# Attention kernel on one core: projection blocks move to odd units, and a fixed set of units copies both halves on ScalarE

## The chip, the core and the metric

The kernel runs on one core of a Trainium2 chip. The time is the device time of one execution in microseconds (us). The five engines work through their own instruction lists in parallel and wait for each other by semaphores: TensorE (PE; its weight loads are listed apart as PEld), VectorE (DVE), ScalarE (ACT), GpSimd (POOL), and SyncE (SP), which issues nearly all DMAs.

## The reference

`x` is 8 × 1024 × 256, `adj` 1024 × 1024. Four residual layers follow one another, each on h = relu(layernorm(x)):

```
x = x + (adj @ h) @ W0 + b0                         # graph layer 0
x = x + norm_adj @ (h @ W1) + b1                    # graph layer 1
x = x + o + layernorm(o),  o = attention_2(h) @ w_proj + b_proj
                                                    # 8 heads of 32, scores masked where adj == 0
x = x + attention_3(h) @ Wo + bo                    # 8 heads of 32, scores + (1 - adj) * -1e9
```

Everything is fp32. Products that need its precision are split into a high and a low part.

## The kernel before, in words

`graph_phase` computes the first two layers and takes the first 480 us; the change does not touch it. `attention_phase` computes the two attention layers in 16 **jobs** (8 batches for each layer). A job has 8 heads of 8 query tiles, so 64 **units** `u`; a unit is one tile of 128 queries against all 1024 keys of one head.

In unit `u` the engines do this, each in the order of its own loop:

- TensorE: `scores` of unit u+2 (two matmuls of 128x512, L720); the unit's **block** if it has one; in even units the `values` of two steps (L751, 16 matmuls that multiply the probabilities of the head before with V); then `transposes` of unit u (L732, eight of 128x128, in two halves of four; each half has its own bank of `pt_ps`).
- VectorE: `masked` for unit u+2 (L939: scores plus mask, and the row's smallest value); the second part of the block (`finish_block`); `copy_pt` of the second half of the transposes (L1014), if ScalarE doesn't do it.
- ScalarE: `exp` for unit u+1 (L870); every 16 units, from u = 7 on, `copy_ot` (L881); `copy_pt` of the first half (L875), and of the second where it is ScalarE's; the first part of the block (`hi_part`).

So each half of `pt_ps` must be copied before the next unit's transposes write it again, and `values` at every eighth unit also needs the first half of the unit before.

A **block** is one piece of projection work that is spread over the units of the attention: `h` and `turn` and `norm` are four transposes; `qk`, `v` and `out` are six matmuls of 512 columns or twelve of 256. All blocks go through one bank, `g_ps`: a block may start when VectorE has finished the one before (`g_free`). For `h`, `turn` and `qk` ScalarE writes the high part first (L852, L864, L860) and VectorE then the low part (L950, L988, L957); `norm`, `v` and `out` have no part on ScalarE. Which unit holds which block is written out by hand in three tables: `EARLY` (the rest of the job before), `MID` (this job), `NEXT` (the job after). The first job has no `EARLY`, the last no `NEXT`. SyncE waits for some blocks as well: the loads of head 4 wait for the fourth `qk` of `MID`, those of the next job's head 0 for the last of `NEXT`.

Before the change ScalarE copies both halves in 19 of the 64 units: those with a `v`, `norm` or `out` block, and of the units without a block those with u % 4 == 3 except u % 16 == 7. In a unit with an `h` or `turn` block the copies stand ahead of the block's own work on ScalarE and VectorE, with any other block behind it.

Of the kernel before, what the change touches and what calls it, by code (L numbers as in the profile page):

```python
# [37 lines left out]
def graph_phase(nc, a, x_mid, mask, shared):  # L38
# [14 lines left out]
    with ExitStack() as ctx:  # L53
# [235 lines left out]
        def _(dve):  # L289
# [124 lines left out]
UNITS = 64  # L414
GROUP = 2
EARLY = [(9, ("norm", 3)), (11, ("turn", 0)), (13, ("out", 0)), (15, ("turn", 1)), (17, ("out", 1)),
         (26, ("turn", 2)), (28, ("out", 2)), (30, ("turn", 3)), (32, ("out", 3))]
MID = [(18, ("qk", 1, 0, 0)), (20, ("qk", 1, 1, 0)), (22, ("qk", 1, 0, 1)), (24, ("qk", 1, 1, 1)),
       (33, ("norm", 0)), (49, ("norm", 1)), (60, ("norm", 2))]
NEXT = [(35, ("h", 0, 0)), (37, ("h", 0, 1)), (40, ("h", 1, 0)), (42, ("h", 1, 1)),  # L420
        (44, ("v", 0)), (45, ("v", 1)), (47, ("v", 2)), (48, ("v", 3)),
        (51, ("qk", 0, 0, 0)), (53, ("qk", 0, 1, 0)), (54, ("qk", 0, 0, 1)), (56, ("qk", 0, 1, 1))]

FIRST = [("h", 0, 0), ("h", 0, 1), ("h", 1, 0), ("h", 1, 1),
         ("qk", 0, 0, 0), ("qk", 0, 1, 0), ("qk", 0, 0, 1), ("qk", 0, 1, 1), ("v", 0), ("v", 1), ("v", 2), ("v", 3)]
# [2 lines left out]
SHORT = ("h", "turn")  # L428
LN_STEP = 16
PER_JOB = len(EARLY) + len(MID) + len(NEXT)  # L430


def blocks_of(first, more):

    table = sorted((EARLY if not first else []) + MID + (NEXT if more else []))
    skip = len(EARLY) if first else 0
    return {step: (skip + i, what) for i, (step, what) in enumerate(table)}


def scalar_halves(table):  # L440


    return {u for u in range(UNITS)
            if (table[u][1][0] in ("v", "norm", "out") if u in table else u % 4 == 3 and u % 16 != 7)}


def attention_phase(nc, a, x_mid, x_mid2, out, mask, shared):
# [11 lines left out]
    with ExitStack() as ctx:  # L459
# [102 lines left out]
        def block_at(job, k):  # L562

            return PER_JOB * job + FIRST_BLOCKS - len(EARLY) + k
# [13 lines left out]
        def tail_block(k):  # L578
            return block_at(JOBS, k) - len(NEXT)

        banks = [g_ps, pt_ps[0], pt_ps[1], ot_ps]

        def bank(k):

            return banks[0 if k is None else k % 4]
# [113 lines left out]
        def _(pe):  # L699
# [108 lines left out]
            def body(job, layer, before, after):  # L808
                table = blocks_of(before is None, after is not None)
                for u in range(UNITS):  # L810
                    if u + 2 < UNITS or after is not None:
                        scores(job, u + 2, UNITS * job + u + 1)
                    if u in table:
                        k, what = table[u]
                        lay = before if (u, what) in EARLY else after if (u, what) in NEXT else layer
                        if what[0] == "norm":
# [25 lines left out]
        @block.scalar  # L842
        def _(act):
            copy = nc.scalar.activation

            def hi_part(n, what, layer, job, k=None, last=False):

                kind, ps = what[0], bank(k)
                if kind == "h":
                    c, nh = what[1:]  # L850
                    act.wait_ge(g_mm, n + 1)
                    copy(hT_hi[:, c, nh * HALF:(nh + 1) * HALF], ps[:], ACT.Relu).then_inc(h_hi_done, 1)  # L852
                elif kind == "qk":
                    g, w, nh = what[1:]
                    if not (g == 0 and job == 0):

                        for s in range(2):
                            act.wait_ge(head_in[s], 128 * (4 * job + 2 * g))
                    act.wait_ge(g_mm, n + 1)
                    copy(st_hi[w][:, nh * HALF:(nh + 1) * HALF], ps[:], ACT.Identity,  # L860
                         bias=b_qk[:, layer, w, g:g + 1]).then_inc(qk_hi_done, 1)
                elif kind == "turn":
                    act.wait_ge(g_mm, n + 1)
                    copy(oT(what[1], last)[0], ps[:], ACT.Copy).then_inc(oT_hi_done, 1)  # L864

            def exp(job, u):
                job, u = (job + 1, u - UNITS) if u >= UNITS else (job, u)

                act.wait_ge(t_done, UNITS * job + u + 1)
                nc.scalar.activation(T[u % RING][:], T[u % RING][:], ACT.Exp, bias=low[:, u % RING:u % RING + 1],  # L870
                                     scale=-1.0, accum_out=rsum[:, u:u + 1]).then_inc(p_done, 1)

            def copy_pt(job, u, half):
                act.wait_ge(tr_done[half], UNITS * job + u + 1)
                copy(pt_of(u, half),  # L875
                     pt_ps[half][:].rearrange("p (k q) -> p k q", k=HT), ACT.Copy).then_inc(pt_done[half], 1)

            def copy_ot(after):

                act.wait_ge(av_done, after)  # L880
                copy(ot_sb[:], ot_ps[:], ACT.Copy).then_inc(ot_done, 1)  # L881

            def weights_hi(layer):
                if layer:
                    act.wait_ge(raw_in, 64)
                raw = raw_weights(layer)

                copy(w_hi[layer][:, :, 0:D], raw[:, :, 0:D], ACT.Copy, scale=-SCALE).then_inc(w_hi_done, 1)
                copy(w_hi[layer][:, :, D:], raw[:, :, D:], ACT.Copy).then_inc(w_hi_done, 1)

            weights_hi(0)
            act.wait_ge(bias_zero, 1)
            for n, what in enumerate(FIRST):
                hi_part(n, what, 0, 0, n)
            weights_hi(1)
            act.wait_ge(bias_done, 1)
            exp(0, 0)

            def body(job, layer, before, after):
                table = blocks_of(before is None, after is not None)  # L900
                for u in range(UNITS):
                    if u + 1 < UNITS or after is not None:
                        exp(job, u + 1)
                    if u % (2 * NT) == NT - GROUP + 1 and (u >= NT or before is not None):
                        copy_ot(UNITS * job + u + GROUP - 1 - NT)
                    halves = (0, 1) if u in scalar_halves(table) else (0,)
                    copy_first = u in table and table[u][1][0] in SHORT
                    if copy_first:
                        for half in halves:
                            copy_pt(job, u, half)  # L910
                    if u in table:
                        k, what = table[u]
                        in_next = (u, what) in NEXT
                        hi_part(block_at(job, k), what, after if in_next else layer, job + 1 if in_next else job)
                    if not copy_first:
                        for half in halves:
                            copy_pt(job, u, half)

            jobs(body)
            copy_ot(UNITS * JOBS)  # L920

            for i in range(2):
                act.wait_ge(head_in[i], 128 * 4 * JOBS)
            for k, what in enumerate(LAST):
                hi_part(tail_block(k), what, 1, None, k, True)
# [3 lines left out]
        def _(dve):  # L929
# [82 lines left out]
            def copy_pt(job, u):  # L1012
                dve.wait_ge(tr_done[1], UNITS * job + u + 1)
                nc.vector.tensor_copy(pt_of(u, 1),  # L1014
                                      pt_ps[1][:].rearrange("p (k q) -> p k q", k=HT)).then_inc(pt_done[1], 1)
# [38 lines left out]
            def body(job, layer, before, after):  # L1054
                table = blocks_of(before is None, after is not None)
                for u in range(UNITS):
                    if u + 2 < UNITS or after is not None:
                        masked(job, u + 2, layer if u + 2 < UNITS else after)
                    copy_first = u in table and table[u][1][0] in SHORT
                    if copy_first and u not in scalar_halves(table):  # L1060
                        copy_pt(job, u)
                    if u in table:
                        k, what = table[u]
                        early, in_next = (u, what) in EARLY, (u, what) in NEXT
                        finish_block(block_at(job, k), what, before if early else after if in_next else layer,
                                     job - 1 if early else job + 1 if in_next else job)
                    if not copy_first and u not in scalar_halves(table):
                        copy_pt(job, u)
                    if after is not None:
                        if LN_STEP <= u < LN_STEP + NT:  # L1070
                            ln_stats(job + 1, u - LN_STEP)
                        if u == LN_STEP + NT:
                            ln_mean(job + 1)
                    if layer != after and after is not None and u >= UNITS - NT + 1:
                        mask3(u - (UNITS - NT + 1))
                        if u == UNITS - 1:
                            mask3(NT - 1)
# [139 lines left out]
```

## Time and profile before

| | us |
|---|---|
| median of 3 runs | 2976.08 (2975.07 to 2977.13) |
| the profiled execution | 2974.42, its span 2972.6 |
| TensorE busy | 2906.1 (98%) |
| VectorE busy | 2401.1 (81%) |
| ScalarE busy | 2126.1 (72%) |
| GpSimd busy | 591.3 (20%) |

The granted TensorE clock has a mean of 0.994 of full speed. The line numbers L... are those of the kernel before. Matmuls are pipelined, so their durations overlap: how long a piece of TensorE's work takes is read from the start of one row to the start of the next. A unit is measured here from the start of its scores (L720) to the start of the next unit's scores. Job 3 runs from 960.53 to 1113.70 us.

### The profile page before, as it was taken

To read this page: it belongs to the slowest core of one execution; us is meant where nothing else is said; L and a number is where in the kernel's file an instruction comes from. 1 tells how busy PE (TensorE), PEld (TensorE's weight loads), DVE (VectorE), ACT (ScalarE), POOL (GpSimd) and SP (SyncE) were. 2 spreads that over 40 slices of the span, in tenths; PEclk is the share of its full clock that TensorE was granted. 3 is DMA by queue.
4 is the path that set the end of the run, shared out by engine and by line. 5 is a ranking of instruction groups with operands and counts; after the bars stand their busy time and mean duration, and the time that the engine had idled before them with its cause. 6 is when DMAs were issued, how large, how long until landed. Compare 5 with 4: busy or idle time off the path is not lost.

```text
span 2972.6 us, 59755 instructions
## 1 busy us (share of the span) xinstructions
PE 2906.1 (98%) x23872; PEld 2199.0 (74%) x23872; DVE 2401.1 (81%) x4427; ACT 2126.1 (72%) x3794; POOL 591.3 (20%) x538
## 2 busy tenths in 40 slices
PE   7999997999999999999999989999999999999998
PEld 6888886777777777777777767777777777777776
DVE  6776775879888888888888878888888787878786
ACT  3000002888888888888888878888888888888887
POOL 2222220105050504131322323010101010101000
PEclk9999998999999999999999999999999999999999
DMA  3001003323233233232323252323233332323232
GB/s 124 29 29 58 29 29 94 70 56 90 69 83 75 71 74 83 65 93 61 96 51 97 67 140 68 90 66 85 65 81 74 82 76 72 87 55 93 65 75 58
DMA packets 123588, 217.19 MB, mean 73 GB/s; under 512 B 20016, under 2 KB 88240, under 8 KB 123312
## 3 DMA queue, kind: packets, MB, share of 16 engines
q1 hardware_dynamic: 122160, 209.14, 28.4%
q0 software_dynamic: 1152, 4.19, 0.6%
q8 instruction: 195, 3.19, 0.4%
q14 instruction: 81, 0.66, 0.1%
HBM read 53.87 MB, written 25.17 MB: 27 GB/s over the span
## 4 chain that ended last, share of the span: by engine, by line
PE 79%; ACT 2%; DVE 1%; DMA 1%; issue 0%; ACTq 0%; DVEq 0%
PE t_pt_ps L732 32%; PE t_ot_ps L751 17%; PE t_s_ps L720 15%; PE t_g_ps L705 4%; PE t_g_ps L706 4%; PE t_g_ps L707 4%; PE t_g_ps L772 1%; PE t_g_ps L776 1%; PE t_g_ps L791 1%; ACT t_T L870 1%; ACT t_PT L875 1%; DMA mask<-in_adj 1%; DVE t_st_lo L957 0%; ACT t_st_hi L860 0%; ACT t_ot L881 0%
## 5 line engine op out<-in xcount | busy, mean ns | idle before, releaser
L939 DVE CUSTOM_DVE_ANT_0 t_T<-t_s_ps,mask 128x1024 f32<-128x1024 f32 x1024 | 1240.6, 1215 | 117.3 <-PE t_s_ps L720 112.5
L870 ACT ACTIVATE t_T<-t_T,t_low 128x1024 f32<-128x1024 f32 x1024 | 1178.8, 1151 | 43.1 <-DVE t_low L939 37.9
L732 PEld LDWEIGHTS t_pt_ps<-t_ident,t_T 128*128 128x128 f32 x8192 | 885.2, 141 | 325.7 <-issue 279.5
L732 PE MATMUL t_pt_ps<-t_ident,t_T 128*128 128x128 f32 x8192 | 1112.6, 279 | 6.3 <-DVE t_PT L1014 4.5
L875 ACT ACTIVATE t_PT<-t_pt_ps 128x512 f32<-128x512 f32 x1324 | 755.9, 596 | 317.9 <-PE t_pt_ps L732 306.7
L720 PE MATMUL t_s_ps<-t_k,t_q 128*128 128x512 f32 x2048 | 729.7, 437 | 8.3 <-DMA t_k<-t_st_lo 7.1
L1014 DVE COPY t_PT<-t_pt_ps 128x512 f32<-128x512 f32 x724 | 499.1, 689 | 196.6 <-PE t_pt_ps L732 194.0
L751 PE MATMUL t_ot_ps<-t_PT,shared 128*32 128x256 f32 x8192 | 549.4, 386 | 8.1 <-ACT t_PT L875 7.9
L751 PEld LDWEIGHTS t_ot_ps<-t_PT,shared 128*32 128x32 f32 x8192 | 215.1, 109 | 255.4 <-issue 128.0
L247 ACT ACTIVATE g_yT_hi<-g_ps 128x512 fp32r<-128x512 f32 x64 | 38.3, 598 | 400.5 <-PE g_ps L187 400.5
L720 PEld LDWEIGHTS t_s_ps<-t_k,t_q 128*128 128x128 f32 x2048 | 310.6, 192 | 9.3 <-DMA t_k<-t_st_lo 7.6
L1108 POOL COPY shared<-shared 128x1024 f32<-128x1024 f32 x16 | 17.0, 1062 | 1263.8 <-PE t_ot_ps L751 1254.0
L185 PE MATMUL g_ps<-g_adjT_hi,g_h_hi 128*128 128x512 f32 x512 | 200.8, 392 | 7.2 <-DVE g_spare L362 5.6
L870 ACT ACTIVATION_READ_ACCUMULATOR t_T<-t_T,t_low 128x1 f32 x1024 | 200.6, 196 | 0.0
L186 PE MATMUL g_ps<-g_adjT_lo,g_h_hi 128*128 128x512 f32 x512 | 200.3, 391 | 0.0
L187 PE MATMUL g_ps<-g_adjT_hi,g_h_lo 128*128 128x512 f32 x512 | 199.9, 390 | 0.0
L957 DVE SCALAR_TENSOR_TENSOR t_st_lo<-t_g_ps,t_b_qk,t_st_hi 128x512 fp32r<-128x512 f32 x125 | 93.8, 750 | 66.1 <-ACT t_st_hi L860 65.1
L860 ACT ACTIVATE t_st_hi<-t_g_ps,t_b_qk 128x512 fp32r<-128x512 f32 x125 | 85.9, 687 | 42.9 <-PE t_g_ps L707 42.9
L185 PEld LDWEIGHTS g_ps<-g_adjT_hi,g_h_hi 128*128 128x128 f32 x512 | 96.7, 189 | 26.8 <-DVE g_spare L362 5.8
L187 PEld LDWEIGHTS g_ps<-g_adjT_hi,g_h_lo 128*128 128x128 f32 x512 | 96.6, 189 | 20.1
L186 PEld LDWEIGHTS g_ps<-g_adjT_lo,g_h_hi 128*128 128x128 f32 x512 | 96.7, 189 | 19.0
L705 PE MATMUL t_g_ps<-t_hT_hi,t_w_hi 128*128 128x512 f32 x250 | 100.7, 403 | 7.6 <-DVE t_st_lo L957 4.8
(185 smaller groups left out, 3158.1 us busy)
## 6 DMA issues: line engine op xcount, KB each, us to landing
t_q<-t_st_hi SPq DMA_DIRECT2D x256, 128.0 KB, 2.3
t_k<-t_st_hi SPq DMA_DIRECT2D x256, 128.0 KB, 2.4
t_k<-t_st_lo SPq DMA_DIRECT2D x256, 128.0 KB, 2.4
t_q<-t_st_lo SPq DMA_DIRECT2D x256, 128.0 KB, 2.4
shared<-x_after_graph_layers SPq DMA_DIRECT2D x8, 1024.0 KB, 6.5
t_xe<-x_after_graph_layers SPq DMA_DIRECT2D x32, 256.0 KB, 3.1
x_after_layer<-t_xe SPq DMA_DIRECT2D x32, 256.0 KB, 2.1
shared<-x_after_layer SPq DMA_DIRECT2D x8, 1024.0 KB, 6.8
```

The costliest lines, as they stand in the source:

```text
L185: mm(out, s_hi, m_hi, start=first, stop=False)
L186: mm(out, s_hi, m_lo, start=False, stop=False)
L187: return mm(out, s_lo, m_hi, start=False, stop=final)
L705: mm(dst, s_hi, m_hi, start=first, stop=False)
L706: mm(dst, s_hi, m_lo, start=False, stop=False)
L720: last = mm(s_ps[u % 2][:, cols], q4[h % 2][:, qt * P:(qt + 1) * P], k4[h % 2][:, cols], start=True, stop=True)
L732: last = nc.tensor.transpose(pt_ps[half][:, i * P:(i + 1) * P], T[u % RING][:, kt * P:(kt + 1) * P], ident[:])
L751: last = mm(ot_ps[j * HD:(j + 1) * HD, h % 2 * 2 * P:(h % 2 + 1) * 2 * P], v_sb[:, kt, h * HD:(h + 1) * HD], probs, start=kt == 0, stop=kt ...
L870: nc.scalar.activation(T[u % RING][:], T[u % RING][:], ACT.Exp, bias=low[:, u % RING:u % RING + 1], scale=-1.0, accum_out=rsum[:, u:u + 1] ...
L875: copy(pt_of(u, half), pt_ps[half][:].rearrange("p (k q) -> p k q", k=HT), ACT.Copy).then_inc(pt_done[half], 1)
L939: nc.vector.tensor_tensor_reduce(out=T[u % RING][:], in0=s_ps[u % 2][:], in1=mask[:, qt, :], scale=1.0, scalar=3.4e38, op0=ALU.add, op1=AL ...
L1014: nc.vector.tensor_copy(pt_of(u, 1), pt_ps[1][:].rearrange("p (k q) -> p k q", k=HT)).then_inc(pt_done[1], 1)
```

## The change

The tables get new unit numbers. Before, 15 of the 28 blocks of a full job stand in even units: 18, 20, 22, 24, 26, 28, 30, 32, 40, 42, 44, 48, 54, 56 and 60. After it three do: 18 (`qk`), 48 (`norm`) and 54 (`qk`). The rule for ScalarE's second halves is replaced by a written set of 32 units. The order within a unit changes too: in even units a block's work stands ahead of the copies on ScalarE and VectorE, whatever its kind; in odd units it stands behind the copies on VectorE, and on ScalarE behind the first copy (`h`, `turn`) or behind all (`qk`).

```diff
-         (26, ("turn", 2)), (28, ("out", 2)), (30, ("turn", 3)), (32, ("out", 3))]
-MID = [(18, ("qk", 1, 0, 0)), (20, ("qk", 1, 1, 0)), (22, ("qk", 1, 0, 1)), (24, ("qk", 1, 1, 1)),
-       (33, ("norm", 0)), (49, ("norm", 1)), (60, ("norm", 2))]
-NEXT = [(35, ("h", 0, 0)), (37, ("h", 0, 1)), (40, ("h", 1, 0)), (42, ("h", 1, 1)),
-        (44, ("v", 0)), (45, ("v", 1)), (47, ("v", 2)), (48, ("v", 3)),
-        (51, ("qk", 0, 0, 0)), (53, ("qk", 0, 1, 0)), (54, ("qk", 0, 0, 1)), (56, ("qk", 0, 1, 1))]
+         (25, ("turn", 2)), (27, ("out", 2)), (29, ("turn", 3)), (31, ("out", 3))]
+MID = [(18, ("qk", 1, 0, 0)), (19, ("qk", 1, 1, 0)), (21, ("qk", 1, 0, 1)), (23, ("qk", 1, 1, 1)),
+       (33, ("norm", 0)), (48, ("norm", 1)), (61, ("norm", 2))]
+NEXT = [(35, ("h", 0, 0)), (37, ("h", 0, 1)), (39, ("h", 1, 0)), (41, ("h", 1, 1)),
+        (43, ("v", 0)), (45, ("v", 1)), (47, ("v", 2)), (49, ("v", 3)),
+        (51, ("qk", 0, 0, 0)), (53, ("qk", 0, 1, 0)), (54, ("qk", 0, 0, 1)), (55, ("qk", 0, 1, 1))]
+BOTH_ON_ACT = {0, 2, 7, 8, 9, 12, 13, 15, 16, 17, 20, 22, 24, 26, 27, 29, 30, 31, 33, 39, 41, 42, 43, 46, 47, 48,
+               50, 54, 56, 58, 61, 63}
...
-def scalar_halves(table):
-    return {u for u in range(UNITS)
-            if (table[u][1][0] in ("v", "norm", "out") if u in table else u % 4 == 3 and u % 16 != 7)}
...
@@ ScalarE, inside the loop over the units
-                    halves = (0, 1) if u in scalar_halves(table) else (0,)
-                    copy_first = u in table and table[u][1][0] in SHORT
...
+                    def hi_of(kinds):
+                        if u in table and table[u][1][0] in kinds:
+                            k, what = table[u]
+                            in_next = (u, what) in NEXT
+                            hi_part(block_at(job, k), what, after if in_next else layer, job + 1 if in_next else job)
+
+                    if u % 2 == 0:
+                        hi_of(SHORT + ("qk",))
+                    copy_pt(job, u, 0)
+                    if u % 2:
+                        hi_of(SHORT)
+                    if u in BOTH_ON_ACT:
+                        copy_pt(job, u, 1)
+                    if u % 2:
+                        hi_of(("qk",))
@@ VectorE, inside the loop over the units
-                    copy_first = u in table and table[u][1][0] in SHORT
-                    if copy_first and u not in scalar_halves(table):
+                    if u % 2 and u not in BOTH_ON_ACT:
                         copy_pt(job, u)
                     if u in table:
                         ...
-                    if not copy_first and u not in scalar_halves(table):
+                    if u % 2 == 0 and u not in BOTH_ON_ACT:
                         copy_pt(job, u)
```

The first place is TensorE from unit 25 of a full job on, where the third `turn` block (four transposes of `t_o`) stands. Before:

```order
L720 MATMUL t_s_ps<-t_k_1,t_q_1 128x512 x2
L732 MATMUL t_pt_ps<-t_ident,t_T 128x128 x8
L720 MATMUL t_s_ps<-t_k_1,t_q_1 128x512 x2
L776 MATMUL t_g_ps<-t_ident,t_o 128x128 x4
L751 MATMUL t_ot_ps<-t_PT,shared 32x256 x8
L732 MATMUL t_pt_ps<-t_ident,t_T 128x128 x8
```

After, from the scores of unit 25 on (the lines of the changed kernel are five lower here):

```order
L715 MATMUL t_s_ps<-t_k_1,t_q_1 128x512 x2
L771 MATMUL t_g_ps<-t_ident,t_o 128x128 x4
L727 MATMUL t_pt_ps<-t_ident,t_T 128x128 x8
L715 MATMUL t_s_ps<-t_k_1,t_q_1 128x512 x2
L746 MATMUL t_ot_ps<-t_PT,shared 32x256 x8
L727 MATMUL t_pt_ps<-t_ident,t_T 128x128 x8
```

The block now stands between scores and transposes of unit 25 and no longer between scores and `values` of unit 26.

The second place is ScalarE in the units 53 and 54, which both hold a `qk` block (`t_st_hi` is its high part, `t_T` the exponential, `t_PT` the copies, `t_ot` the copy of `ot`). Before:

```order
L870 ACTIVATE t_T,t_rsum<-t_T,t_low 128x1024
L860 ACTIVATE t_st_hi<-t_g_ps,t_b_qk 128x512
L875 ACTIVATE t_PT<-t_pt_ps 128x512
L870 ACTIVATE t_T,t_rsum<-t_T,t_low 128x1024
L860 ACTIVATE t_st_hi<-t_g_ps,t_b_qk 128x512
L875 ACTIVATE t_PT<-t_pt_ps 128x512
L870 ACTIVATE t_T,t_rsum<-t_T,t_low 128x1024
L881 ACTIVATE t_ot<-t_ot_ps 128x512
```

After:

```order
L865 ACTIVATE t_T,t_rsum<-t_T,t_low 128x1024
L870 ACTIVATE t_PT<-t_pt_ps 128x512
L855 ACTIVATE t_st_hi<-t_g_ps,t_b_qk 128x512
L865 ACTIVATE t_T,t_rsum<-t_T,t_low 128x1024
L855 ACTIVATE t_st_hi<-t_g_ps,t_b_qk 128x512
L870 ACTIVATE t_PT<-t_pt_ps 128x512 x2
L865 ACTIVATE t_T,t_rsum<-t_T,t_low 128x1024
L876 ACTIVATE t_ot<-t_ot_ps 128x512
```

In unit 53 the copy now stands ahead of the block's high part; in unit 54 the high part stays ahead and two copies follow instead of one.

The third place is VectorE in unit 53 and at the start of unit 54 (`t_st_lo` is the low part of a `qk` block, `ISA` the mask operation). Before:

```order
L957 SCALAR_TENSOR_TENSOR t_st_lo<-t_g_ps,t_b_qk,t_st_hi 128x512
L1014 COPY t_PT<-t_pt_ps 128x512
L939 ISA t_T,t_low<-t_s_ps,mask 128x1024
L939 ISA t_low 128x1
L957 SCALAR_TENSOR_TENSOR t_st_lo<-t_g_ps,t_b_qk,t_st_hi 128x512
L1014 COPY t_PT<-t_pt_ps 128x512
```

After:

```order
L1014 COPY t_PT<-t_pt_ps 128x512
L957 SCALAR_TENSOR_TENSOR t_st_lo<-t_g_ps,t_b_qk,t_st_hi 128x512
L939 ISA t_T,t_low<-t_s_ps,mask 128x1024
L939 ISA t_low 128x1
L957 SCALAR_TENSOR_TENSOR t_st_lo<-t_g_ps,t_b_qk,t_st_hi 128x512
```

The copy of unit 53 has moved ahead of the block's low part, and unit 54 has no copy on VectorE.

## Rows read from the trace of the kernel before

**Rows 1.** Busy times of the engines in job 3 (us, instructions, then clock and DMA)
```profile
960.53:1113.73 153.20, 152.43 (x1348) 112.68 (x1346) 130.69 (x242) 129.02 (x233) 43.20 (x43) 1.00 0.32 77
```
**Rows 2.** Timeline, TensorE's scores of units 2, 3, 4 (start, us, engine, instruction)
```profile
964.49 0.71 PE L720 MATMUL t_s_ps<-t_k,t_q 128*128 128x512 f32 x2
...
966.98 0.71 PE L720 MATMUL t_s_ps<-t_k,t_q 128*128 128x512 f32 x2
...
968.42 0.71 PE L720 MATMUL t_s_ps<-t_k,t_q 128*128 128x512 f32 x2
```
**Rows 3.** Timeline, TensorE's scores of units 10 and 12 (`turn` in 11)
```profile
981.07 0.71 PE L720 MATMUL t_s_ps<-t_k,t_q 128*128 128x512 f32 x2
...
985.33 0.71 PE L720 MATMUL t_s_ps<-t_k,t_q 128*128 128x512 f32 x2
```
**Rows 4.** Timeline, scores of units 24 (`qk`), 26 (`turn`) and 28
```profile
1016.00 0.70 PE L720 MATMUL t_s_ps<-t_k,t_q 128*128 128x512 f32 x2
...
1021.31 0.70 PE L720 MATMUL t_s_ps<-t_k,t_q 128*128 128x512 f32 x2
...
1025.67 0.71 PE L720 MATMUL t_s_ps<-t_k,t_q 128*128 128x512 f32 x2
```
**Rows 5.** Timeline, scores of units 44, 45 (`v`), 46, and 51 (`qk`), 52
```profile
1062.25 0.71 PE L720 MATMUL t_s_ps<-t_k,t_q 128*128 128x512 f32 x2
...
1066.16 0.71 PE L720 MATMUL t_s_ps<-t_k,t_q 128*128 128x512 f32 x2
...
1068.92 0.71 PE L720 MATMUL t_s_ps<-t_k,t_q 128*128 128x512 f32 x2
...
1082.34 0.72 PE L720 MATMUL t_s_ps<-t_k,t_q 128*128 128x512 f32 x2
...
1085.08 0.70 PE L720 MATMUL t_s_ps<-t_k,t_q 128*128 128x512 f32 x2
```
**Rows 6.** Timeline, all engines in units 53 and 54 (brackets: idle before, releaser)
```profile
1089.51 1.04 PE L732 MATMUL t_pt_ps<-t_ident,t_T 128*128 128x128 f32 x8
...
1089.79 0.69 ACT L860 ACTIVATE t_st_hi<-t_g_ps,t_b_qk 128x512 fp32r<-128x512 f32 x1 [0.66 <-PE t_g_ps L707]
...
1090.30 0.70 PE L720 MATMUL t_s_ps<-t_k,t_q 128*128 128x512 f32 x2
1090.37 0.59 ACT L875 ACTIVATE t_PT<-t_pt_ps 128x512 f32<-128x512 f32 x1
1090.51 0.75 DVE L957 SCALAR_TENSOR_TENSOR t_st_lo<-t_g_ps,t_b_qk,t_st_hi 128x512 fp32r<-128x512 f32 x1 [0.84 <-ACT t_st_hi L860]
...
1091.32 0.50 PE L705 MATMUL t_g_ps<-t_hT_hi,t_w_hi 128*128 128x512 f32 x1 [0.32 <-DVE t_st_lo L957]
...
1094.60 0.60 ACT L875 ACTIVATE t_PT<-t_pt_ps 128x512 f32<-128x512 f32 x1 [0.82 <-PE t_pt_ps L732]
...
1094.75 0.71 PE L720 MATMUL t_s_ps<-t_k,t_q 128*128 128x512 f32 x2
...
1095.09 1.14 ACT L870 ACTIVATE t_T<-t_T,t_low 128x1024 f32<-128x1024 f32 x1
```
**Rows 7.** Timeline, ScalarE's first copy of unit 7 and `values` of unit 8
```profile
976.80 0.59 ACT L875 ACTIVATE t_PT<-t_pt_ps 128x512 f32<-128x512 f32 x1
...
977.44 1.07 PE L751 MATMUL t_ot_ps<-t_PT,shared 128*32 128x256 f32 x16 [0.44 <-ACT t_PT L875]
```
**Rows 8.** Timeline, both halves copied by ScalarE in unit 9 (behind a block) and 28
```profile
980.28 1.04 PE L732 MATMUL t_pt_ps<-t_ident,t_T 128*128 128x128 f32 x8
...
980.91 1.09 ACT L875 ACTIVATE t_PT<-t_pt_ps 128x512 f32<-128x512 f32 x2
...
1029.39 1.09 ACT L875 ACTIVATE t_PT<-t_pt_ps 128x512 f32<-128x512 f32 x2 [1.00 <-PE t_pt_ps L732]
...
1030.13 1.06 PE L732 MATMUL t_pt_ps<-t_ident,t_T 128*128 128x128 f32 x8
```
**Rows 9.** DMA issues of the mask's reload between jobs 7 and 8
```profile
mask<-in_adj POOLq DMA_DIRECT2D x8, 512.0 KB, 10.5
```

More of the change, by code:

```diff
@@ L905, in body @@
                         copy_ot(UNITS * job + u + GROUP - 1 - NT)
-                    halves = (0, 1) if u in scalar_halves(table) else (0,)
-                    copy_first = u in table and table[u][1][0] in SHORT
[L908 to L917, printed above, removed]
+                    def hi_of(kinds):
[12 more added lines that the diff above has]
+                        hi_of(("qk",))
             jobs(body)
```

## The prediction

> **What bounds the kernel now.** I read the busy times of one whole job first, then TensorE's rows unit by unit, then the rows of all engines at the places where TensorE waits. In [rows 1] TensorE is busy for 152.43 of the 153.20 us of job 3, VectorE for 130.69 and ScalarE for 129.02. The jobs 1 to 14 are alike, but for 7 and 8 in which the mask is reloaded; so all of them are paced by TensorE, and the others have 22 and 24 us to spare. A job is 64 units: an even unit holds scores, two `values` and transposes, an odd one scores and transposes. A plain even unit takes 2.49 us from its scores to the next, a plain odd one 1.44, a plain pair 3.93 [rows 2].
>
> **Part 1: blocks move from even to odd units.** What a block costs depends on where it stands. A `turn` in an odd unit makes its pair 4.26 us [rows 3], so it costs 0.33; in an even unit the pair is 4.36 [rows 4], so 0.43. A `qk` in an even unit makes the pair 5.31 [rows 4], or +1.38; an odd unit with one takes 2.74 against 1.44 [rows 5], or +1.30. A `v` costs 3.91 − 2.49 = 1.42 in an even unit and 2.76 − 1.44 = 1.32 in an odd one [rows 2, 5]. So a move saves 0.10 for the short ones and `v`, 0.08 for `qk`, and for `out` I take the same. To odd units go four `qk`, two `out`, two `turn`, two `h`, one `norm` and two `v`; one `norm` goes to an even one (49 to 48): 6 × 0.08 + 5 × 0.10 + 2 × 0.10 − 0.10 = 1.08 us per full job. No row shows a longer row of odd blocks than two units, so a move might save nothing or twice as much; the rows at hand give the middle.
>
> **Part 2: what TensorE waits for.** Three waits are left in a full job.
> - Unit 8. `values` waits for ScalarE's copy of unit 7 [rows 7], which stands behind the copy of `ot`: the copy starts at 976.80, the matmul at 977.44 with 0.44 of wait shown, and the unit is about 0.5 longer than a plain one. Units 7 and 8 hold no block before or after, and the first half is copied at the same place. Unchanged.
> - Unit 40. The same geometry, but today the 0.43 of the `h` block lies between scores and `values` and hides all but some 0.08 of the wait. Moved to unit 39 it delays that unit's transposes by only 0.33, so 0.18 is left: +0.10. At 24 and 56 the block in front is a `qk` of 1.3, and nothing is left, as now.
> - Unit 54. Two `qk` blocks follow each other here (53, 54) in one bank, so the second waits until VectorE is through with the first. Today [rows 6]: the transposes of unit 53 start at 1089.51, ScalarE takes the block's high part at 1089.79, ahead of its copy (1090.37), VectorE takes the low part 0.72 later (1090.51), and the next block starts 0.81 after that (1091.32). Without the wait it would stand 0.55 behind the scores of 1090.30, so 0.47 is waited. In the changed kernel an odd unit's `qk` part comes behind its copy on ScalarE, and the copy needs four transposes that stand behind the block on TensorE. Behind a block the copy starts 0.63 after the transposes (980.28 to 980.91 [rows 8]), here at 1090.14; the high part follows 0.49 later (the distance from 1094.60 to 1095.09 [rows 6]) at 1090.63, the low part at 1091.35, the block at 1092.16. That is 0.84 us later than now, and unit 54 goes from 4.45 (1090.30 to 1094.75) to 5.29.
>
> Behind that block stand `values` and transposes of unit 54, the scores of 57 and the `qk` of 55, and all come 0.84 later. The block of 55 needs no more: from the block of 54 its bank is free after some 1.6 for the block, 0.28, 0.72 and 0.81, or 3.4 us, and TensorE comes to it after 3.43 + 0.55 = 3.98 (1091.32 to 1094.75, and its scores). The other odd `qk` (19, 21, 23, 51) get their high part late too, but the next block is two units off, 3.8 us for a chain of 2.65 (0.63 + 0.49 + 0.72 + 0.81). The DMA queue waits for the blocks of units 23 and 55 before it loads heads 4 and 0; these were 24 and 56, so it is earlier. The step at 54 costs 0 only if the high part passed a waiting copy, which the rows deny: the exponential of 1095.09 stood behind a copy that waited 0.82 (1094.60). VectorE's own copy of unit 53 now stands ahead of the low part; were it not over by then, another 0.6 would come on top, 1.5 in all. I take 0.84. A full job changes by -1.08 + 0.84 + 0.10 = -0.14 us, fourteen of them by -2.0.
>
> **Part 3: thirteen more second halves on ScalarE.** It copies both halves in 32 units instead of 19. At 0.49 each this is 6.4 us per job, of 24 it has to spare; where, matters. A pair holds two exponentials of 1.14 (1095.09) and two copies of 0.49, 3.26 us, with two more copies 4.24. A plain pair is 3.93. In the new table a pair with two extra copies holds a block in every full job (8/9, 12/13, 16/17, 26/27, 30/31, 42/43, 46/47), so it lasts 4.26 or more: it just fits. Tightest is an even unit with no block behind it. [rows 8] show one of today: two copies from 1029.39, the next unit's transposes at 1030.13 with no wait; its second copy starts at 1029.88, must be 0.64 ahead of the second half (976.80 to 977.44 [rows 7]), at 1030.52, and that half starts about 0.43 behind 1030.13, at 1030.56. So 0.04 is left, and I cost part 3 at nothing in full jobs. If the cover is gone, it is up to 0.1 in each of 17 even units, 1.7 us per job.
>
> The Trainium skill (Advanced Engine Details and Errata, "The Read-Write Bubble") says that instructions of ScalarE and VectorE do not overlap at their ends, which leaves a bubble between them. By it a copy would take its whole 0.60, a pair with two extra ones 2 × 1.14 + 4 × 0.60 = 4.68, and seven pairs per job would be 0.42 late: 47 us in sixteen jobs, near 3021. The rows speak against it: 0.49 from one to the next, for a copy of 0.60, and two copies in 1.09 (1029.39).
>
> **The first and the last job.** The set is fixed now, while these have fewer blocks. Job 0 lacks the early ones, and `values` up to unit 7, so ScalarE is its bound there: two more copies are 1.0 us, and its five double pairs without a block up to 0.2 each, another 1.0. With 0.7 saved and 0.94 lost as above, +2.2. Job 15 lacks the last ones: 0.6 saved, two pairs 0.2 late each: -0.2. Where the mask is reloaded (jobs 7, 8) TensorE stands still until DMAs land that took 10.5 us [rows 9], set off by work whose order stays: 0, within 1 us.
>
> **Sum.** -2.0 + 2.2 − 0.2 = 0.0 us. The profiled execution's own time is 2974.42 (its span 2972.6), 1.66 below the median of the runs, 2976.08. So 2974.4 on its scale and 2976 as a median.
>
> **Rivals.**
> 1. The wait at 54 does not grow, or the moves save 0.15 and not 0.10. For it: ScalarE is idle around 54, and the odd units' blocks stand between like rows. Against it: the order in which ScalarE takes them. The first form gives 15 × 0.84 = 12.6 us less, 2963.5; the second 15 × 0.5 = 8 less, 2968; both 2956.
> 2. Slower: ScalarE is late with the second half in even units where it copies both. It decides from 0.04 us on where no block follows (units 0, 2, 56, 58), from 0.4 to 1.4 where one does. If all 17 lost 0.05, 16 × 17 × 0.05 = 13.6 more: 2989.5; 0.1 each makes 3003. For it: the pairs that just fit. Against it: [rows 8].
> 3. The change does not do what it says: the blocks stand in odd units, but unit 54 takes the gain back. That is the forecast itself, with part 3 as work moved beside TensorE's.
>
> **How the numbers follow.** About 0.2% (6 us) is what a measurement of this kernel can tell from no change. A full job must be off by 0.4 us to get there, and my terms for one are good to some 0.2 to 0.3. The forecast gets 0.51. Rival 1 gets 0.27, all of it faster; rival 2 gets 0.22, with 0.02 of it for the rule on the bubble. The likeliest case alone lies between 2971 and 2981. To hold eight in ten the range takes in the first form of rival 1 and the milder one of rival 2: 2962 to 2990.
>
> **What would show it.** Full jobs of 152.8 to 153.3 us; pairs with an odd `turn` or `h` of 4.26; unit 54 at 5.3 with its block waiting for VectorE's low part; no wait of TensorE for second copies in full jobs; job 0 some 2 us longer. Wrong would be a unit 54 below 4.7, or plain pairs above 3.95.

## The result, and the profile after

| | us | runs |
|---|---|---|
| before | 2975.05 (2973.66 to 2978.96) | 12 |
| changed | 2967.97 (2966.1 to 2972.39) | 12 |

The ratio is 0.9975, with a 95% interval of 0.9967 to 0.9982: faster by 0.25%. That is inside the range, but the likeliest case was "no change" (2971 to 2981), and the changed kernel lies just below it. The profiled execution of the changed kernel has a span of 2965.0 us, 7.6 below the one before.

Where these 7.6 are is read job by job, each from the scores of its unit 1 to those of the next job's unit 1 (job 15 to its last scores), and then unit by unit:

| part | before | changed | difference |
|---|---|---|---|
| 12 full jobs (1 to 6, 9 to 14), each | 153.19 | 152.90 | -0.29, together -3.4 |
| jobs 7 and 8 (reload of the mask) | 160.32 + 159.82 | 155.36 + 159.11 | -5.7 |
| job 0 | 145.11 | 146.25 | +1.1 |
| job 15 | 133.33 | 132.99 | -0.3 |
| unit 1 of job 0 starts at | 511.5 | 512.1 | +0.6 |

The last line can't be put down to the change: a second profile of each kernel (e7, e4) has 512.8 and 511.5.

The busy times of job 3 answer to [rows 1]:

```profile
961.62:1114.52 152.90, 151.19 (x1347) 113.15 (x1346) 123.38 (x229) 135.18 (x246) 43.19 (x43) 1.00 0.32 75
```

VectorE lost 7.3 us per job and ScalarE took on 6.2 (129.02 to 135.18), but TensorE still sets the pace. The scores of units 1, 2, 24, 25 and 26 answer to [rows 4] and [rows 2]:

```profile
964.14 0.71 PE L715 MATMUL t_s_ps<-t_k,t_q 128*128 128x512 f32 x2
...
965.55 0.71 PE L715 MATMUL t_s_ps<-t_k,t_q 128*128 128x512 f32 x2
...
1018.15 0.70 PE L715 MATMUL t_s_ps<-t_k,t_q 128*128 128x512 f32 x2
...
1020.63 0.71 PE L715 MATMUL t_s_ps<-t_k,t_q 128*128 128x512 f32 x2
...
1022.40 0.71 PE L715 MATMUL t_s_ps<-t_k,t_q 128*128 128x512 f32 x2
```

The pair 24/25 now holds a `turn` in its odd unit and takes 4.25 us; a `turn` in an even unit made 4.36. But unit 1 takes 1.41, and a plain odd unit took 1.44 [rows 2]: that was not foreseen. Unit 54 answers to [rows 6], in all engines:

```profile
1089.71 1.04 PE L727 MATMUL t_pt_ps<-t_ident,t_T 128*128 128x128 f32 x8
...
1090.34 0.60 ACT L870 ACTIVATE t_PT<-t_pt_ps 128x512 f32<-128x512 f32 x1 [0.84 <-PE t_pt_ps L727]
1090.50 0.70 PE L715 MATMUL t_s_ps<-t_k,t_q 128*128 128x512 f32 x2
...
1090.84 0.68 ACT L855 ACTIVATE t_st_hi<-t_g_ps,t_b_qk 128x512 fp32r<-128x512 f32 x1
...
1091.55 0.75 DVE L957 SCALAR_TENSOR_TENSOR t_st_lo<-t_g_ps,t_b_qk,t_st_hi 128x512 fp32r<-128x512 f32 x1
...
1092.36 0.50 PE L700 MATMUL t_g_ps<-t_hT_hi,t_w_hi 128*128 128x512 f32 x1 [1.16 <-DVE t_st_lo L957]
...
1095.80 0.71 PE L715 MATMUL t_s_ps<-t_k,t_q 128*128 128x512 f32 x2
```

From the transposes 0.63 to the copy, 0.50 to the high part, 0.71 to the low part, 0.81 to the block. The wait shown grew from 0.32 to 1.16, the unit from 4.45 to 5.30. The list of waits of the whole execution has it 15 times (its total in us, how often, the longest), once in each job but the last:

```profile
PE t_g_ps L700 <- DVE t_st_lo L957: 17.4, 15, 1.2
```

The reload of the mask is where most of the gain is. GpSimd issues its eight DMAs behind `masked` of the units 56 to 63 of job 7, and `masked` of the next job waits for them. Windows of ten us from the first issue on, of before and then of the changed kernel (the last three columns are the granted clock, the share of the DMA engines and GB/s):

```profile
1706.08:1716.08 10.00, 10.00 (x94) 6.73 (x85) 8.05 (x14) 8.28 (x15) 2.74 (x4) 1.00 0.59 163
1716.08:1726.08 10.00, 6.85 (x58) 4.96 (x57) 6.15 (x12) 6.89 (x14) 2.28 (x4) 0.98 1.03 204
1726.08:1736.08 10.00, 8.79 (x63) 5.74 (x63) 7.23 (x12) 5.35 (x10) 1.03 (x1) 0.68 1.05 244
```
```profile
1705.35:1715.35 10.00, 10.00 (x95) 6.95 (x94) 6.55 (x11) 8.58 (x16) 2.35 (x4) 1.00 0.55 141
1715.35:1725.35 10.00, 8.74 (x84) 5.88 (x76) 8.62 (x16) 8.07 (x15) 2.92 (x5) 1.00 1.00 287
1725.35:1735.35 10.00, 6.71 (x58) 4.63 (x54) 5.13 (x9) 5.73 (x11) 0.29 (x1) 1.00 1.05 259
```

In both the DMA engines are full from the second window on, but in the second window of the changed kernel they move 287 GB/s and not 204; over the thirty us it is 229 and 204 in the mean. The fourth tile's issue on GpSimd and the mask operation that waits for it on VectorE, before:

```profile
1715.23 1.03 POOL L1155 DMA_DIRECT2D mask<-in_adj  x1 [3.03 <-DVE t_low L939]
...
1726.10 0.69 DVE L1020 TENSOR_SCALAR mask<-mask 128x1024 f32<-128x1024 f32 x1 [3.84 <-DMA mask<-in_adj]
```

and in the changed kernel:

```profile
1714.89 1.03 POOL L1154 DMA_DIRECT2D mask<-in_adj  x1 [0.98 <-DVE t_low L939]
...
1722.98 0.69 DVE L1020 TENSOR_SCALAR mask<-mask 128x1024 f32<-128x1024 f32 x1 [1.34 <-DMA mask<-in_adj]
```

10.9 us from issue to use became 8.1. The eighth tile is issued only when the fourth has let VectorE go on (2.13 us behind its use in both), so it comes sooner as well. It is what VectorE waits for last, before and then in the changed kernel:

```profile
1739.12 0.69 DVE L1020 TENSOR_SCALAR mask<-mask 128x1024 f32<-128x1024 f32 x1 [2.96 <-DMA mask<-in_adj]
```
```profile
1735.38 0.69 DVE L1020 TENSOR_SCALAR mask<-mask 128x1024 f32<-128x1024 f32 x1 [3.53 <-DMA mask<-in_adj]
```

Both kernels started unit 1 of job 7 at 1575.74, so 3.7 of the 5.7 us are won by then. Most of the rest is TensorE's clock. It fell from 2.4 to 1.2 GHz while TensorE stood idle behind this wait, and in the kernel before it stayed there twice as long as in the changed one (the third number from the end is the granted clock):

```profile
1739.39:1746.22 6.83, 4.60 (x26) 2.69 (x27) 5.23 (x9) 2.97 (x5) 0.00 (x0) 0.50 0.03 11
```
```profile
1737.08:1740.49 3.41, 3.22 (x19) 1.30 (x20) 3.02 (x7) 2.85 (x5) 0.00 (x0) 0.50 0.00 0
```

Before, the clock was at 1.2 GHz once more, from 1725.74 to 1732.57, but that stretch ended while the eighth tile was still on its way. So did TensorE's own longest waits for a DMA, which the profile puts down to the last load of `t_k` for the next job's head 0 (4.36 us up to 1727.29, and 1.26 up to 1723.70 in the changed kernel). The median time of the eight from issue to landing, in answer to [rows 9]:

```profile
mask<-in_adj POOLq DMA_DIRECT2D x8, 512.0 KB, 7.5
```

### The profile page after: what moved, and what is told of

It is laid out like the page before. It is cut to its first block, busy times and chain, and to the rows that moved or that the text cites. A ratio compares the mean times of both kernels' runs of the same rounds, so it can differ in the third digit from the quotient of the medians.

```text
span 2965.0 us, 59755 instructions
## 1 busy us (share of the span) xinstructions
PE 2886.2 (97%) x23872; PEld 2205.8 (74%) x23872; DVE 2283.8 (77%) x4215; ACT 2225.7 (75%) x4006; POOL 590.6 (20%) x538
## 4 chain that ended last, share of the span: by engine, by line
PE 77%; ACT 5%; DVE 1%; DMA 1%; issue 0%; ACTq 0%; DVEq 0%
PE t_pt_ps L727 31%; PE t_ot_ps L746 17%; PE t_s_ps L715 14%; PE t_g_ps L700 4%; PE t_g_ps L701 4%; PE t_g_ps L702 4%; ACT t_PT L870 2%; ACT t_T L865 2%; PE t_g_ps L767 1%; PE t_g_ps L771 1%; PE t_g_ps L786 1%; DMA mask<-in_adj 1%; ACT t_ot L876 1%; DVE t_st_lo L957 0%; ACT t_st_hi L855 0%
## 5 line engine op out<-in xcount | busy, mean ns | idle before, releaser
L727 PE MATMUL t_pt_ps<-t_ident,t_T 128*128 128x128 f32 x8192 | 1097.1, 277 | 3.0 <-ACT t_PT L870 1.7
L727 PEld LDWEIGHTS t_pt_ps<-t_ident,t_T 128*128 128x128 f32 x8192 | 897.8, 141 | 268.2 <-issue 226.2
L870 ACT ACTIVATE t_PT<-t_pt_ps 128x512 f32<-128x512 f32 x1536 | 870.0, 599 | 247.4 <-PE t_pt_ps L727 231.6
L1014 DVE COPY t_PT<-t_pt_ps 128x512 f32<-128x512 f32 x512 | 353.1, 690 | 200.8 <-PE t_pt_ps L727 200.6
L715 PEld LDWEIGHTS t_s_ps<-t_k,t_q 128*128 128x128 f32 x2048 | 310.2, 192 | 10.9 <-DVE t_low L939 4.8
```

Source lines behind the costliest of these rows:

```text
L715: last = mm(s_ps[u % 2][:, cols], q4[h % 2][:, qt * P:(qt + 1) * P], k4[h % 2][:, cols], start=True, stop=True)
L727: last = nc.tensor.transpose(pt_ps[half][:, i * P:(i + 1) * P], T[u % RING][:, kt * P:(kt + 1) * P], ident[:])
L870: copy(pt_of(u, half), pt_ps[half][:].rearrange("p (k q) -> p k q", k=HT), ACT.Copy).then_inc(pt_done[half], 1)
L1014: nc.vector.tensor_copy(pt_of(u, 1), pt_ps[1][:].rearrange("p (k q) -> p k q", k=HT)).then_inc(pt_done[1], 1)
```

## The experiments

All were timed beside the kernel before on the same chip, except e7. "Stall of the reload" is the length of jobs 7 and 8 together less two full jobs of the same profile; it was 13.8 before and 8.7 in the changed kernel.

**e1: only the tables.** The tables of the changed kernel stand in the kernel before; its rule for second halves and its order stay.

```diff
-         (26, ("turn", 2)), (28, ("out", 2)), (30, ("turn", 3)), (32, ("out", 3))]
+         (25, ("turn", 2)), (27, ("out", 2)), (29, ("turn", 3)), (31, ("out", 3))]
```

> Only the three tables are those of the changed kernel; the rule for second halves and the order within a unit stay as before. Theory (each move saves 0.08 to 0.10 us, and the order within odd units is what costs 0.84 in unit 54): full jobs of 152.2 us (153.2 before, 152.9 changed), unit 54 at 4.45 as before and unit 40 at 2.67; the time some 15 us below the kernel before, 2960, and 7 below the changed kernel. Rival (the wait in unit 54 comes from the neighbourhood 53, 54, 55 in the new table, not from the order): unit 54 at 5.3, full jobs of 153.0, 2972.

2960.68 us, ratio 0.9949 (0.9936 to 0.9963). Full jobs of 152.33 (two of the twelve 152.63), unit 54 at 4.46, unit 40 at 2.68, stall of the reload 10.1. The theory holds: the moves alone are worth 0.85 us per job, and the other two parts of the change give 0.57 of it back. One thing was not in it: units 24 and 56 take 2.57 and not 2.49.

**e2: only the set.**

```diff
 def scalar_halves(table):
-    return {u for u in range(UNITS)
-            if (table[u][1][0] in ("v", "norm", "out") if u in table else u % 4 == 3 and u % 16 != 7)}
+    return BOTH_ON_ACT
```

> Only the set of units in which ScalarE copies both halves is the changed kernel's; tables and order are those of before. Theory (a blockless odd unit behind an even unit whose two halves ScalarE copies takes 1.41 instead of 1.44, as units 29 and 61 do before and 1, 3, 57 and 59 in the changed kernel): nine or ten more such units, full jobs of 152.9, and with 1.1 us more in job 0 a time of 2972. Rival (the set only moves idle time): full jobs of 153.2, time 2975 or up to 1 more. Rival (ScalarE comes late): waits of TensorE for L875, full jobs above 153.5.

2986.55 us, ratio 1.0036 (1.0024 to 1.0048): slower. The third theory has the length of the full jobs right, but not the wait. Units 21, 23, 25, 27, 31, 43 and 55 do fall to 1.41, so the 0.03 are real. But units 28, 32 and 44 take 4.23 to 4.25 and not 3.86 to 3.90, and full jobs 154.0 to 154.1. The rows of units 26 to 28:

```profile
1026.93 1.09 ACT L877 ACTIVATE t_PT<-t_pt_ps 128x512 f32<-128x512 f32 x2 [0.51 <-PE t_pt_ps L734]
...
1027.90 0.60 ACT L866 ACTIVATE t_oT_hi<-t_g_ps 128x512 fp32r<-128x512 f32 x1
1028.38 1.16 ACT L872 ACTIVATE t_T<-t_T,t_low 128x1024 f32<-128x1024 f32 x1
1028.49 0.72 PE L722 MATMUL t_s_ps<-t_k,t_q 128*128 128x512 f32 x2
1028.54 0.69 DVE L990 TENSOR_TENSOR t_oT_lo<-t_g_ps,t_oT_hi 128x512 fp32r<-128x512 f32 x1 [2.07 <-ACT t_oT_hi L866]
...
1029.29 0.39 PE L707 MATMUL t_g_ps<-t_w_hi,t_oT_hi 128*128 128x256 f32 x1
```

In unit 26 (a `turn`) both copies now stand ahead of the high part on ScalarE, which comes at 1027.90; VectorE's low part comes at 1028.54, and TensorE, which reaches the next block 0.55 behind the scores of 1028.49, can start it only at 1029.29. The late releaser is once more ScalarE's order ahead of a block, as in unit 54, and no wait for copies. The set was only fit for its own tables. The stall of the reload fell all the same, to 8.1, and the fourth tile needs 8.3 us.

**e3: tables and set, but the old order within a unit.**

> Tables and set of the changed kernel, but the order within a unit of the kernel before: a qk block's high part ahead of the copies on ScalarE, its low part ahead of the copy on VectorE. Theory: unit 54 falls from 5.30 to about 4.46, full jobs from 152.9 to 152.1, 15 x 0.84 = 12.6 us less than the changed kernel, 2955. Rival (copies that come later in odd units cost TensorE elsewhere what 54 gains): full jobs stay at 152.8 to 153.0 and the time at 2968.

2967.98 us, ratio 0.9973 (0.9963 to 0.9983); full jobs of 152.87, stall of the reload 7.1. The theory falls, although its own part is there: unit 54 is back at 4.45. But units 24 and 56 take 2.77 (2.48 in the changed kernel), and unit 41 takes 2.00 (1.77): +0.81 together. The rows of units 23 and 24:

```profile
1017.10 0.59 ACT L883 ACTIVATE t_ot<-t_ot_ps 128x512 f32<-128x512 f32 x1
1017.10 1.03 PE L734 MATMUL t_pt_ps<-t_ident,t_T 128*128 128x128 f32 x8
1017.58 0.70 ACT L862 ACTIVATE t_st_hi<-t_g_ps,t_b_qk 128x512 fp32r<-128x512 f32 x1
...
1018.15 0.61 ACT L877 ACTIVATE t_PT<-t_pt_ps 128x512 f32<-128x512 f32 x1
...
1018.81 1.06 PE L753 MATMUL t_ot_ps<-t_PT,shared 128*32 128x256 f32 x15 [0.22 <-ACT t_PT L877]
```

ScalarE is late by the copy of `ot`, then takes the high part, and `values` of unit 24 wait for the copy behind it. In the changed kernel the copy comes first:

```profile
1017.36 1.03 PE L727 MATMUL t_pt_ps<-t_ident,t_T 128*128 128x128 f32 x8
1017.38 0.58 ACT L876 ACTIVATE t_ot<-t_ot_ps 128x512 f32<-128x512 f32 x1
...
1017.99 0.60 ACT L870 ACTIVATE t_PT<-t_pt_ps 128x512 f32<-128x512 f32 x1
...
1018.78 1.07 PE L746 MATMUL t_ot_ps<-t_PT,shared 128*32 128x256 f32 x16
```

So "copy first" is right in units 23 and 55 and wrong in 53; a rule for all odd `qk` units must pay one or the other. The 0.23 of unit 41 have another source: in unit 39, with an `h` block, the old order puts both copies ahead of the high part (it starts at 1055.37), the changed one puts it between them (1054.84).

**e4: the changed kernel again.**

> The changed kernel once more, unaltered, for a second profile: full jobs again 152.9. If the 5 us that job 7 lost come from the change, job 7 takes 155 to 156 us again; if they are chance in how the mask's DMAs land, it lies elsewhere between 155 and 160.

2970.26 us, ratio 0.9979 (0.997 to 0.9988). Full jobs of 152.93; job 7 at 155.27, job 8 at 160.67, a stall of 10.1. The fourth tile needs 8.0 us from issue to use, as in the first profile (8.1). Job 7 repeats, job 8 is 1.5 us longer. Of these 1.2 lie behind the last tile, where the clock is now at 1.2 GHz for 6.8 us and not for 3.4.

**e5 and e6: both kernels without the reload.** The DMAs, the mask operations and the wait for them are taken out, so that the last eight jobs work with the first mask:

```diff
-                if layer != after and after is not None:
-                    load_mask3()
```

> The kernel before without the reload of the mask between jobs 7 and 8 (no DMAs, no mask operations; jobs 8 to 15 work with the first mask): jobs 7 and 8 fall from 160.3 and 159.8 to 153.2 like the others, so 13.7 us less than the kernel before, 2961.

2961.11 us, ratio 0.9953 (0.994 to 0.9967). Jobs 7 and 8 at 153.20 and 153.16. As expected: the reload costs 14.3 us.

> The changed kernel without the reload, left out in the same way. Theory (the reload's stall is shorter by 5.7 us in the changed kernel, and the rest of the gain is 0.29 per full job): jobs 7 and 8 at 152.9, and against the kernel before without reload only 14 x 0.29 - 0.5 = some 3 us less, 2958. Rival (the gain is all in the ordinary jobs and the reload costs the same): 7 us less, 2954.

2959.47 us, ratio 0.995 (0.9937 to 0.9964). Jobs 7 and 8 at 152.91 and 152.89. Without the reload the change is worth 1.6 us in the medians and 2.3 in the spans (2958.7 and 2956.4). The two intervals against the kernel before overlap almost wholly, so in the timings this is no difference that could be told. About five of the seven us thus need the reload, as the first theory said.

**e7: the kernel before again.**

> The kernel before, unaltered, for a second profile: jobs 7 and 8 at 160.3 and 159.8 us if the reload's stall is a property of the kernel; several us away from that if it varies from execution to execution.

One execution, 2977.26 us. Jobs 7 and 8 at 158.73 and 161.33, a stall of 13.7; the fourth tile needs 10.7 us. How the stall is divided between the two jobs varies, its sum and the tile's time do not.

**e8: one entry of one table.**

```diff
-(54, ("qk", 0, 0, 1)), (56, ("qk", 0, 1, 1))]
+(54, ("qk", 0, 0, 1)), (55, ("qk", 0, 1, 1))]
```

> The kernel before with one entry changed: the last qk block of the job after stands in unit 55 instead of 56. Theory (where the blocks around the triggers of the mask's reload stand decides how long its DMAs and the loads of head 0 take together): full jobs 0.08 shorter by the move and longer by a copy of unit 55 that stands behind the high part on ScalarE, 153.2 in sum; but the fourth mask tile lands some 8 us after its issue instead of 10.8, and jobs 7 and 8 are 3 to 5 us shorter together: 2971. Rival (it needs the other moves as well, or the set): jobs 7 and 8 stay at 320 us together, time 2975.

2973.93 us, ratio 0.9993 (0.9984 to 1.0002): the timing can't tell it from no change. The profile can: full jobs of 153.18, the fourth tile 8.4 us from issue to use, jobs 7 and 8 at 155.72 and 161.07, a stall of 10.4. So in the profile this entry alone brings most of the difference. It is not needed for it: in e2 the block stands in 56 as before. All profiles with the reload, split at the use of the last tile (in us; the two parts add up to the stall but for rounding):

| kernel | last `qk` in unit | fourth tile, issue to use | stall up to the last tile | stall behind it | time at 1.2 GHz behind it |
|---|---|---|---|---|---|
| before, e7 | 56 | 10.9, 10.7 | 10.2, 9.6 | 3.6, 4.2 | 6.8, 6.8 |
| changed, e4 | 55 | 8.1, 8.0 | 6.7, 7.0 | 1.9, 3.1 | 3.4, 6.8 |
| e1 | 55 | 7.9 | 6.4 | 3.7 | 6.8 |
| e2 | 56 | 8.3 | 7.1 | 0.9 | 0 |
| e3 | 55 | 8.1 | 6.2 | 0.9 | 0 |
| e8 | 55 | 8.4 | 7.1 | 3.3 | 6.6 |
| e9 | 55 | 8.9 | 7.7 | 3.1 | 6.8 |
| e10 | 55 | 8.9 | 8.0 | 2.1 | 3.4 |
| e11 | 57 | 8.6 | 8.4 | 0.8 | 0 |
| e12 | 55 | 8.4 | 6.6 | 2.1 | 3.4 |

Up to the last tile only the kernel before is slow, by 1.2 to 4.0 us. The part behind it follows the clock, and that differs between two profiles of the changed kernel.

**e9: high part first in unit 53 alone.** All else as in the changed kernel; on VectorE the low part of unit 53 stands ahead of its copy as well.

```diff
-                    if u % 2 == 0:
+                    if u % 2 == 0 or u == 53:
                         hi_of(SHORT + ("qk",))
...
-                    if u % 2:
+                    if u % 2 and u != 53:
                         hi_of(("qk",))
```

> The changed kernel, but in unit 53 alone the qk block's high part stands ahead of ScalarE's copy and its low part ahead of VectorE's copy, as before the change. Theory (0.84 us are lost in unit 54 because of this order, while in units 23 and 55 the same order saves 0.29 each in units 24 and 56): unit 54 at 4.45, units 24 and 56 stay at 2.48, full jobs of 152.05, 15 x 0.85 = 12.7 us less than the changed kernel, about 2956. Rival (the units 53 to 56 hang together, so that 55 is late instead): full jobs of 152.9 as in the changed kernel or in the one with the old order.

2957.22 us, ratio 0.9935 (0.9921 to 0.9948). Full jobs of 152.06, unit 54 at 4.47, units 24 and 56 at 2.48. Its rows:

```profile
1087.41 1.03 PE L727 MATMUL t_pt_ps<-t_ident,t_T 128*128 128x128 f32 x8
...
1087.69 0.69 ACT L855 ACTIVATE t_st_hi<-t_g_ps,t_b_qk 128x512 fp32r<-128x512 f32 x1 [0.49 <-PE t_g_ps L702]
...
1089.22 0.51 PE L700 MATMUL t_g_ps<-t_hT_hi,t_w_hi 128*128 128x512 f32 x1 [0.32 <-DVE t_st_lo L957]
```

1.81 us from the transposes to the next block, where the changed kernel has 2.65. The time is 10.8 to 13 us below the changed kernel's two medians; 12.7 were expected.

**e10: the exponential behind the copies in units 7 and 39.** All else as in e9, but for the second halves of these two units, which go to VectorE (7 and 39 leave the set; the cut does not show it).

```diff
+                    late_exp = u in (7, 39)
-                    if u + 1 < UNITS or after is not None:
+                    if not late_exp and (u + 1 < UNITS or after is not None):
                         exp(job, u + 1)
...
                     copy_pt(job, u, 0)
+                    if late_exp:
+                        exp(job, u + 1)
```

> As the run before, and in units 7 and 39 ScalarE takes the copy of ot and the copy of the first half ahead of the exponential (whose result is needed last); the second halves of these two units go to VectorE. Theory (values in units 8 and 40 wait for ScalarE's order alone): unit 8 falls from 3.00 to 2.49 and unit 40 from 2.67 to 2.49, 0.7 per job, 10 to 11 us less, about 2945. Rival (the exponential of unit 8 becomes late for its transposes): unit 8 at 2.6 to 2.9 with a wait for L865 or unit 9 longer, 2950 to 2956.

2958.60 us, ratio 0.9941 (0.9928 to 0.9955): no gain over e9. Unit 8 falls to 2.48 and unit 40 to 2.49, as expected. But unit 41 takes 2.50 and not 1.77:

```profile
1051.15 1.14 ACT L865 ACTIVATE t_T<-t_T,t_low 128x1024 f32<-128x1024 f32 x1
...
1052.29 0.58 ACT L847 ACTIVATE t_hT_hi<-t_g_ps 128x512 fp32r<-128x512 f32 x1
...
1052.90 0.69 DVE L953 SCALAR_TENSOR_TENSOR t_hT_lo<-t_g_ps,t_hT_hi 128x512 fp32r<-128x512 f32 x1 [1.11 <-ACT t_hT_hi L847]
...
1053.51 1.22 DVE L942 CUSTOM_DVE_ANT_0 t_T<-t_s_ps,mask 128x1024 f32<-128x1024 f32 x1
...
1054.63 1.42 PE L727 MATMUL t_pt_ps<-t_ident,t_T 128*128 128x128 f32 x8 [0.18 <-ACT t_PT L870]
```

The `h` block's high part now waits for the exponential, VectorE stands idle for 1.11 before the low part, its mask operation and copy of unit 40 follow late, and the transposes of unit 41 stretch to 1.42. Neither theory named this.

**e11: the last `qk` blocks in 51, 53, 55, 57.** All else as in e10, but unit 53 has the copy first again.

> As the run before, but the last four qk blocks stand in 51, 53, 55, 57, so that no two follow each other, and all odd ones have the copy first again. Theory: unit 54 falls from 4.45 to 2.49 and unit 57 rises by 1.3, 0.66 per job less. Rival (the loads of head 0, which start only behind the last block, land too late for the scores in unit 62): a wait for a DMA of t_k or t_q in unit 62 of 1 us or more per job, which takes the gain back or more, 2945 to 2960.

2957.91 us, ratio 0.9942 (0.9929 to 0.9956): no gain over e10. Unit 54 takes 2.48 and unit 57 takes 2.74, as expected; full jobs vary between 152.01 and 152.83. The rival is right in kind: in the list of waits

```profile
PE t_s_ps L715 <- DMA t_k<-t_st_lo: 17.9, 16, 7.0
```

of which one is the 7.0 in unit 62 of job 7 and one, of 2.8, lies ahead of job 0. The other 14 are 0.3 to 1.2 us each, 8.2 together, in front of the scores of unit 62, and unit 61, which ends with them, takes 2.37 and not 1.78 in the median.

**e12: as e9, and unit 7 of e10.** Here too the second half of unit 7 goes to VectorE.

> As e9, with e10's change in unit 7 alone; unit 39 is again as in e9 (exponential first, both halves on ScalarE). Theory (e10 gained 0.52 in unit 8 and 0.18 in unit 40, and lost 0.73 in unit 41, since the h block's high part of unit 39 came behind the exponential): unit 8 at 2.49, 40 at 2.67, 41 at 1.78, full jobs of 151.54, 16 x 0.52 = 8 us below e9, 2949. Rival (the gain of unit 8 is lost elsewhere too): full jobs of 152.06, 2957.

2949.82 us, ratio 0.9915 (0.9902 to 0.9929), the fastest of all. Unit 8 at 2.49, 40 at 2.68, 41 at 1.77, full jobs of 151.54. The row of job 3:

```profile
959.07:1110.62 151.55, 151.12 (x1348) 113.16 (x1346) 123.84 (x230) 134.54 (x245) 43.18 (x43) 1.00 0.32 78
```

TensorE is busy in all but 0.43 us of it. It beats the kernel before by 25 us and the changed kernel by 18 to 20.

## Why the prediction was right or wrong

**Part 1, moves.** Right. Odd `turn` pairs take 4.25 to 4.26, odd `qk` units 2.74, odd `v` units 2.75. e1 measures moves together with the +0.10 of unit 40 and small waits in 24, 54 and 56 at -0.86, which leaves -1.15 for the moves; I had -1.08 and +0.10.

**Part 2, waits.** Right to 0.01: unit 54 at 5.30 for 5.29, unit 40 at 2.67, unit 8 at 3.00. e9 shows that the order in unit 53 makes the 0.84. My text left out what the same order is good for: it said of units 24 and 56 only that "nothing is left, as now". That is true because of "copy first"; e3 shows 0.29 each without it.

**Part 3, second halves.** Right in that full jobs pay nothing for them (transposes wait for L870 for 1.7 us in the whole execution, six times), but "at nothing" missed a gain: a blockless odd unit behind an even one whose halves ScalarE copies is 0.03 shorter. Four such units (1, 3, 57, 59) make 0.12, which is most of the way from the -0.14 that I had for a full job to the -0.29 measured. That the set must fit the tables (e2) I had not considered.

**The first and last job.** Job 0 grew by 1.1 and not 2.2, job 15 fell by 0.3 and not 0.2. The term of job 0 was twice too large. Its double pairs do come late: units 11, 15 and 29 are 0.27 longer and unit 32 is 0.51. But the 1.0 for two more copies at its start was argued, not read: units 0 to 9 are 0.1 shorter together.

**The step that failed** is "set off by work whose order stays: 0, within 1 us", for the reload. It is -5.7 us with the ordinary 0.6 of two jobs in it. The order of the triggers did stay, but the blocks between them moved, and the tiles' DMAs landed sooner: the fourth needed 2.8 us less, and the last tile was in use 3.7 us earlier in its job. The rest is TensorE's clock behind that tile, a term that the prediction didn't have; e4 shows that the change does not bring this part each time. e5 and e6 show that some five of the seven us hang on the reload. Moving one block (e8: 56 to 55) makes the DMAs faster, but so does the set alone, with the block in 56 (e2). Why they are slow in the kernel before is thus open. In e8 and the changed kernel the third tile is issued 7.2 to 8.0 us behind the first and not 5.6, which might keep it clear of the loads of head 0; but in e2 it is 5.5 and the fourth tile still needs only 8.3. This was not tested apart.

The time fell in the range because the range was wide. For full jobs the forecast was close (-0.14 for -0.29); some five of the 7 us came from a term put at nothing, and no rival named it.

**The rivals.** The wait at 54 grew as forecast, and the moves save some 0.10 each (-1.15 in sum) and not 0.15, so rival 1 was wrong in both forms; that its side came true was luck. Rival 2 was wrong: no late second half in the full jobs. The rule on the bubble of the Trainium skill (Advanced Engine Details and Errata, "The Read-Write Bubble"), as the prediction turned it into a price, did not hold: it is 0.50 us from the start of a copy of 0.60 to the start of the next instruction (1090.34 to 1090.84), and not 0.60.

## What to carry to other kernels

When blocks are spread over a pipelined loop, price each by what it stands between, and check for every queue whether its own order fits each place: one rule for all odd units cost 0.84 us at one of them and saved 0.29 at two others, and the exception was worth some 12 us (10.8 to 13.0). If a transfer on the path shares the DMA engines with others, treat it as a term with an uncertainty of its own even when the change touches neither its size nor its order, and read the granted clock behind the wait before you credit the change with all of the difference.

## What the runs showed of the hardware

- At a full share of the DMA engines (1.00 to 1.05) the rate was 204 GB/s in one kernel and 287 in the other, in ten us of the same reload. A full share is thus no measure of what gets through.
- TensorE's clock was granted at 1.2 instead of 2.4 GHz once or twice around the reload in every profile that has it, and not at all there in the two without (e5, e6). Two matmuls of 128x512 took 1.22 us at the lower level (at 1737.27 in the changed kernel) and 0.71 at the higher. In the stretch before it fell there (1732.8 to 1737.1) TensorE stood idle. Behind the last tile such a stretch cost 1.0 to 3.4 us (that part takes 0.8 to 0.9 without one and 1.9 to 4.2 with one). In e2 it came earlier, and VectorE still waited 1.53 us for the last tile behind it.
- TensorE's odd unit takes 1.41 or 1.44 us with the same instructions, depending on whether ScalarE or VectorE copies the second half of the unit before. e2 changes only who copies: eleven units went from 1.44 to 1.41, and unit 61 from 1.41 to 1.44; what makes it was not tested.
